# Spreading the one-hot fetch of an edge pass over TensorE's step, and reading a register earlier on VectorE

## What is computed

```python
kj = k[src] + e                              # e = edge_attr @ We
alpha = sum(q[dst] * kj, axis=-1) / sqrt(C)
m = segment_max(alpha, dst)
a = exp(alpha - m[dst]);  a = a / (segment_sum(a, dst)[dst] + 1e-16)
out = segment_sum(a[..., None] * (v[src] + e), dst) + x @ Ws + bs
```

## Time and profile before

| | |
|---|---|
| median of 3 runs | 6994.35 us (6991.68 to 7013.82) |
| the profiled execution | 6985.68 us, span 6984.0 us |
| busy in the span | PE 86%, PEld 67%, DVE 79%, ACT 40%, POOL 63% |
| mean granted TensorE clock | 0.839 of 2.4 GHz |

### The profile page before, as it was taken

One profiled execution on the slowest core, in us unless ns is written; L12 is line 12 of the kernel. 1 busy time (PEld: TensorE's weight loads), 2 busy tenths in 40 slices (PEclk: granted clock), 3 DMA queues, 4 the chain that ended last, 5 costly groups with the idle time before them and its releaser, 6 DMA issues. The chain is left out here.

```text
span 6984.0 us, 195570 instructions
## 1 busy us (share of the span) xinstructions
PE 6011.7 (86%) x49413; PEld 4686.6 (67%) x49413; DVE 5529.8 (79%) x18582; ACT 2823.3 (40%) x12163; POOL 4374.1 (63%) x4735
## 2 busy tenths in 40 slices
PE   7996888888888887888888888888888888888887
PEld 5775666666666666666666666666666666666666
DVE  6557888888788888887888888888888888888887
ACT  3224444444444444444444444445333333333332
POOL 1225666666666665666666666665766666666665
PEclk9997888888888888888888888888888888888887
DMA  4553333333333333333333333333333333333332
GB/s 129 159 157 94 90 91 91 91 90 91 90 89 91 89 90 95 92 91 90 91 91 91 89 92 88 91 90 92 96 91 91 92 91 91 91 91 91 91 91 73
DMA packets 732932, 662.41 MB, mean 95 GB/s; under 512 B 421004, under 2 KB 558158, under 8 KB 732878
## 3 DMA queue, kind: packets, MB, share of 16 engines
q1 hardware_dynamic: 555242, 315.06, 16.9%
q0 software_dynamic: 148544, 293.76, 16.9%
q10 hardware_dynamic: 29092, 52.97, 2.5%
HBM read 639.39 MB, written 21.78 MB: 95 GB/s over the span
## 5 line engine op out<-in xcount | busy, mean ns | idle before, releaser
L1906 POOL DMA_INDIRECT Gall<-KV,sdn x4440 | 4223.4, 951 | 2013.5 <-issue 1258.9
L1211 ACT ACTIVATE vals<-vj,vals 128x32 f32<-128x32 f32 (+1 forms) x7960 | 1796.3, 313 | 19.3
L1204 ACT ACTIVATE vals<-dd 128x16 f32<-128x16 f32 (+1 forms) x606 | 131.8, 217 | 3386.8 <-DVE dd L1019 3332.2
L1151 PE MATMUL pG<-KVH,ohB 128*128 128x512 f32 (+1 forms) x2586 | 1269.6, 494 | 28.5 <-DVE cont L884 17.5
L1151 PE MATMUL pG<-KVH,ohA 128*128 128x512 f32 (+1 forms) x2613 | 1206.3, 465 | 24.6 <-DVE lm L878 4.8
L1151 PE MATMUL pG<-KVL,ohB 128*128 128x512 f32 (+1 forms) x2586 | 1210.7, 472 | 0.0
L1151 PE MATMUL pG<-KVL,ohA 128*128 128x512 f32 (+1 forms) x2613 | 1147.0, 443 | 0.0
L1151 PEld LDWEIGHTS pG<-KVH,ohB 128*128 128x128 f32 x2586 | 644.2, 249 | 222.6 <-issue 79.5
L1144 PE MATMUL pY<-O,vals 128*66 128x42 f32 (+1 forms) x10576 | 788.2, 238 | 0.0
L1151 PEld LDWEIGHTS pG<-KVH,ohA 128*128 128x128 f32 x2613 | 609.1, 233 | 201.9 <-issue 79.8
L1144 PEld LDWEIGHTS pY<-O,vals 128*66 128x66 f32 (+1 forms) x10576 | 711.5, 144 | 46.5 <-ACT vals L1218 34.4
(11 more groups left out here) (266 smaller groups left out, 8613.3 us busy)
## 6 DMA issues: line engine op xcount, KB each, us to landing
db<-D SPq DMA_DIRECT2D x606, 256.0 KB, 3.7
ea<-in_ea SPq DMA_DIRECT2D x606, 128.0 KB, 2.1
Gall<-KV,sdn POOLq DMA_INDIRECT x4440
db<-D ACTq DMA_DIRECT2D x202, 256.0 KB, 3.6
qw<-QT SPq DMA_DIRECT2D x1818, 5.2 KB
dr<-in_dr SPq DMA_DIRECT2D x1212, 4.0 KB
ea<-in_ea SPq DMA_DIRECT2D x202, 64.0 KB, 3.5
sdn<-in_sdn SPq DMA_DIRECT2D x606, 12.0 KB
```

What stands on the lines that cost most here:

```text
L1151: p = e.matmul(pG[:, 0:128 * m], table[:, n, :], half[:, 4 * q:4 * q + m, :].rearrange("p t c -> p (t c)"), start=n == 0 and h == 0, stop= ...
L1204: return e.activation(vals[u][:, :, 64:64 + H], dd[:, :, 0:H], ACT.Exp, scale=scale)
L1211: i = e.activation(vals[u][:, j, C * h:C * h + C], vj[u][:, j, C * h:C * h + C], ACT.Identity, scale=vals[u][:, j, 64 + h:65 + h])
L1906: e.indirect_dma_start(G[u][:, j, :], None, kvtab, bass.IndirectOffsetOnAxis(ap=sdn[u][:, j:j + 1], axis=0)).then_inc(s_g[u], 16)
```

## The change

The products of a fetch are cut into up to five groups a step, and a function `feed(e, at, n)` issues group n at five places: ahead of `Fb`, behind `q`, behind `agg`, behind `e`, and behind `aT`. The numbers of quads in them are in `MEALS`: step A 2, 2, 2, 1, 2; step B 0, 0, 3, 2, 3; step C 2, 2, 1, 0, 4. The share of the `ohA` fetch that step B does falls from 9 quads to 8, and step C does 5 in place of 4 of it; `v_oh` follows. VectorE's register read of `base` and the wait for `aT` are parted: the read now stands behind `oh` and ahead of `X`, the wait stays ahead of `facc`.

```diff
-    CUT_A, CUT_B = QUADS - QUADS // 3, QUADS // 3
+    CUT_A, CUT_B = QUADS - QUADS // 3 - 1, QUADS // 3
+    MEALS = {"A": [2, 2, 2, 1, QUADS - CUT_B - 7], "B": [0, 0, 3, 2, CUT_A - 5],
+             "C": [2, 2, QUADS - CUT_A - 4, 0, CUT_B]}
...
-                "P": ["B Fb", "A q", "Z gq", "D agg7", "B Mn", "Z e", "A aT", "A gp", "B Me"],
+                "P": ["B Fb", "A q", "D agg7", "Z gq", "B Mn", "Z e", "A aT", "A gp", "B Me"],
...
+        def feed(e, s, n):
+
+            if not made(s):
+                return None
+            kind = "A" if s.slot == slot_A else "B" if s.slot == slot_B else "C"
+            meals = MEALS[kind]
+            if not meals[n]:
+                return None
+            if sum(meals[:n]) == 0:
+                after(e, "V", "oh", s)
+                hold(e)
+                if kind == "B" and picks(s):
                     after(e, "V", "sel", s)
                     hold(e)
+            if kind == "C" and n == 4:
+                after(e, "V", "early", s + 1)
+                hold(e)
+                return fetch(e, ohB, 0, CUT_B)
+            f = sum(meals[:n]) + {"A": CUT_B, "B": 0, "C": CUT_A}[kind]
+            return fetch(e, ohB if kind == "A" else ohA, f, f + meals[n])
...
+            if "D" in on:
+                base_of[dt.c] = base_at(e, dt)
             if "B" in on:
                 v_X(e, bt).then_inc(pV, 1)
...
-                v_facc(e, dt, pFacY).then_inc(pV, 1)
+                after(e, "P", "aT", dt + 3)
+                v_facc(e, dt, pFacY, preset=True).then_inc(pV, 1)
...
+            feed(e, at, 0)
             if "B" in on:
                 p_Fb(e, bt).then_inc(pP, 1)
...
-            if picked_early(zt):
-                p_gq(e, zt).then_inc(pP, 1)
+            feed(e, at, 1)
...
                 p_agg(e, dt, T - 1).then_inc(pP, 1 if picked_early(zt) else 2)
...
+            fed = feed(e, at, 2)
+            if picked_early(zt):
+                fed.then_inc(pP, 1)
...
+            feed(e, at, 3)
             if "A" in on:
                 p_aT(e, at).then_inc(pP, 1)
...
+            fed = feed(e, at, 4)
             if made(at):
-                p_gp(e, at).then_inc(pP, 1)
+                fed.then_inc(pP, 1)
```

More of the change, by code:

```diff
@@ L1604, in tensor_step @@
                 missing(e, "P", t, "q", "q")
-            if picked_early(zt):
-                p_gq(e, zt).then_inc(pP, 1)
-            elif "D" not in on:
-                missing(e, "P", t, "gq", "gq")
+            feed(e, at, 1)
             if "D" in on:
@@ L1617, in tensor_step @@
                 p_agg(e, dt, T - 1).then_inc(pP, 1 if picked_early(zt) else 2)
-            else:
-                missing(e, "P", t, "agg7", "agg7")
+            elif picked_early(zt):
+                missing(e, "P", t, "agg7", "agg7")
+            else:
+                missing(e, "P", t, "agg7", "gq")
+            fed = feed(e, at, 2)
+            if picked_early(zt):
+                fed.then_inc(pP, 1)
             if "B" in on:
```

## The result

The changed kernel takes 6326.5 us (6323.5 to 6331.4, four runs) beside 7002.8 us of the kernel before: a ratio of 0.9035, 95% interval 0.9016 to 0.9054. On some chips every kernel, the one before too, takes 45 to 48% longer; a run from there is told with a reference from the same chip, and no floor is read from it.

A forecast was written before the change was run, and what follows sets the result against it. VectorE and TensorE waiting for each other in turn set the 30.72 us period; GpSimd's gathers come next at 27.8. 202 x (30.72 - 27.8) = 590 us off 6985.7, plus 8.7, gives 6405 us, range 6340 to 6810.

The forecast's parts named there:

- the pick: VectorE's step B pick (L906) waits for the last product of step A's lump; 2.0 us a period, expected to go.
- `Fb` in step C: `Fb` comes late behind step B's lump, so VectorE waits ahead of `fhi`; price 0 or 2.3 us a period by the clock.
- the register read: VectorE's read of the base ahead of `facc`, 0.45 us a step; hidden behind `oh` it saves 1.35 us a period.
- The first factor: The 202 periods, each taken as 30.72 us before the change, in the saving 202 x (30.72 - 27.8).
- The second: GpSimd's floor after the change: 22 gathers a period at 1.263 us each, 27.8 us.
- The clock: TensorE's granted clock, expected at a mean of 0.90 to 0.97, falling in part of the periods between steps A and B.
- the low clock: Rival: small bunches don't raise TensorE's clock, it needs 33.8 us a period and is the bound; 7620 us, chance 0.11.
- half the gain: Rival: step B runs low and its wait returns, 6525 us, or 6810 with the read unhidden; 6530 to 6960 has chance 0.22.
- no change: Rival: delays of `Fb` or `aT` by the groups give back what the smaller lump yields; 6990 us, chance 0.03.
- The fourth: Rival: GpSimd isn't the floor; its inherent gap of 0.30 us makes 27.5 us a period, 6345 us, the least seen.

The follow-up runs named there:

- more_again: Changed kernel with one gather more a period (tile 3 of slot C's blocks again, into its own buffer), 23 in all: 6576.4 us beside 6997.1 of the kernel before.
- read_only: Kernel before with only VectorE's register read moved behind `oh`: 6954.6 us, ratio 0.9922.
- spread_B: Changed kernel with only step B's groups kept; step A in one lump behind `aT`, step C nearly as before; read moved: 6680.1 us, ratio 0.953.
- spread_A: Changed kernel with only step A's groups kept; step B in one lump behind `aT`, step C nearly as before; read moved: 6618.5 us, ratio 0.9443.
- after_again: Changed kernel unaltered, run once more on a chip where every kernel is slower: 9729 us, 0.955 of the kernel before there.

## Why the prediction was wrong, point by point

*The bound and the mechanism were right.* The period of the kernel before held 4.65 us of VectorE's waits for TensorE and for the read; the waits named (the pick, `Fb` in step C, the register read) went, but for 0.9 us; GpSimd's gathers came next, without a gap, and `more_again` shows with the right price that they set the period.

*The step that failed: two terms of the sum were mis-sized, and the range had room for neither.* The forecast was 202 x (30.72 - 27.8) = 590 us.

- The first factor: "A period of three steps is therefore 614.35 / 20 = 30.72 us" was read from twenty periods of the third layer and set for all 202. The mean over the three layers is (30.99 + 30.95 + 30.72) / 3 = 30.89. 202 x 0.17 = 34 us. The first two layers work on two heads (`alpha` is 128x16 there and 128x8 in the third), which the prediction never asked about.
- The second: "22 x 1.263 = 27.8 us". The 0.314 us of idle time is a mean that holds gaps of up to 0.9 us, and those were no part of the issue rate: when GpSimd is the bound its longest gap is 0.3. Measured are 27.57 us in the mean, 1.253 a gather. 202 x 0.23 = 46 us.

34 + 46 = 80 of the 86 us by which the saving between the medians, 676, exceeds 590. That the miss is 79 is in part luck: the forecast set out from 6985.7 + 8.7 = 6994.4 us, and the kernel before took 7002.8 this time. The lower end came from "22 x 1.25 = 27.5 us, 6345 us", the right rate set against the wrong period of before; with 30.89 it gives 6985.7 - 202 x 3.39 + 8.7 = 6310 us, and the result would have lain inside.

*The register read* was hidden behind `oh` as said, 0.45 us to 0.0 three times in a period. It was right to count it only against VectorE's floor: alone it is worth 53 us, and not the 270 expected of `read_only` later.

*The pick and `Fb`*: both waits fell, from 2.0 to 0.4 and from 1.3 to 0.3 us a period. The prediction priced them as separate sums; `spread_B` shows that the one grows when the other goes (3.9 us ahead of the pick), and `spread_A` that both shrink together. That cost nothing here, since both go.

*The clock*: 0.938, within the 0.90 to 0.97 forecast. Where it would fall was wrong: not between steps A and B but at the start and the end of step C, behind a wait for `Me` or for the pick. The prediction weighed a rule of the Trainium skill ("TensorE: Matmul & The Clock Gate", in "Loop structure matters more than you think"): matmuls are to stay back to back, and a long wait between them lets the clock fall. It took from this that the change would take away what raises the clock, and that didn't come true: without the lumps the clock rose from 0.839 to 0.938, and groups of two to eight products with other work between them kept 1.00 over 25.6 us in which TensorE was busy 22.5. On waits the trace agrees in kind, though they are short here: the falls come behind or in waits of TensorE, 1.28 us in the one form shown, 0.92 and 1.93 us in the other. How much of the gain is the clock's is open: TensorE's busy time is 2.4 us a period less, but no run holds the clock and changes the order, or the reverse.

*The rivals*: the low clock, half the gain and no change didn't come. The fourth named 22 x 1.25 = 27.5 us as the least that the period could be, 6345 us; the period is 27.57, and the right count of microseconds stood there against the wrong period of before.

## What to carry to other kernels

Where two engines hand a loop to and fro, try to spread a long lump over the places where its engine waits; and price the change by the next floor, not by the waits that it removes: taking one wait away alone gave 53 us where its length would give 270. Read a loop's period in every layer whose shapes differ before multiplying it by a count. The floor of an engine that is bound by issuing is the usual gap between its instructions, not the mean gap of a run in which it had slack. A register read behind a long instruction of its own engine can be hidden: here it went from 0.45 us to 0.0.

## What the runs showed of the hardware that was not expected

The kernel before has the same period, 30.72 us, in its third layer and, with the read moved, in all three, although 1.35 us of idle time had been taken out of VectorE's path. In that third layer each of sixty periods has two low stretches of the clock, and they begin at the same two places of the period to within 0.4 us. It looks as if the loop and the clock's changes hold each other in step. That would be a second reason why the register read alone gave nothing in that layer, beside the wait for the lumps, and part of why spreading them gave so much; no run tests it.

And the same program took 6997 us and some 10340 us on one chip at two times. The time is not in longer instructions of GpSimd or ScalarE (in `after_again` a gather takes 950 ns and `vals` 313, as on the first chip), but in idle time in front of instructions that wait for nothing the profile shows, or for ids. TensorE's products do take longer there, 572 ns in place of 462 for the costliest group, at a granted clock of 0.73 in place of 0.938.
